# Edge passes of a graph network in pairs of groups, destination addresses loaded mid-step; unpacking's comparisons cut into pieces

## The reference, cut to what matters

```python
for l in range(5):                                   # first network
    h = leaky(x @ W1[l] + b1[l]) @ W2[l] + b2[l]     # a 3125 x 64 table
    e = leaky(edge_attr @ We1[l] + be1[l]) @ We2[l] + be2[l]   # 100000 x 64
    agg = segment_sum(h[src] * e * dot_scale[l], dst, num_segments=n)
    x = layernorm(x + agg * res_w[l]) * ln_g[l] + ln_b[l]
...
msgs = relu(x[src] + edge_inputs)                    # last network
agg = segment_sum(msgs, dst, num_segments=n)
```

## Time and profile before

| | |
|---|---|
| median of 3 runs | 7217.39 us (7210.43 to 7232.62) |
| the profiled execution | 7237.52 us |
| its span | 7235.9 us, mean granted TensorE clock 0.875 |
| unpacking, first to last addition | 1567.4 to 2429.3 us |
| second edge pass, first gather to last scatter | 3031.0 to 3471.1 us |
| last edge pass | 6788.9 to 7215.5 us |

### The profile page before, as it was taken

The page is one execution under the profiler, slowest core; times in us unless marked ns, Lnnn a source line. Parts: engine busy times, 40 slices in busy tenths (PEclk is TensorE's granted clock), DMA queues, the critical chain, the costliest instruction groups (busy, mean ns, idle before and its releaser), DMA issues. The chain is left out here.

```text
span 7235.9 us, 277379 instructions
## 1 busy us (share of the span) xinstructions
PE 5529.5 (76%) x87510; PEld 4589.8 (63%) x87511; DVE 5239.2 (72%) x14769; ACT 2923.1 (40%) x5054; POOL 3176.5 (44%) x4856
## 2 busy tenths in 40 slices
PE   4888888835555477777777777776989998999777
PEld 3666666624444277677676676776957775777676
DVE  7555555589999788788788787887755554555698
ACT  2444444424444434344343343444643332333343
POOL 1777777767777355355354453551000000000254
PEclk9899999955555599899899898997679998999999
DMA  2776766622222488588587786884531111111497
GB/s 73 197 200 200 198 200 200 196 61 73 72 72 72 167 218 228 151 229 229 151 228 202 182 227 157 225 228 148 191 120 64 64 61 41 65 64 65 115 235 203
DMA packets 1403299, 1098.89 MB, mean 152 GB/s; under 512 B 1012405, under 2 KB 1171820, under 8 KB 1393466
## 3 DMA queue, kind: packets, MB, share of 16 engines
q1 hardware_dynamic: 787494, 772.05, 34.5%
q0 software_dynamic: 224768, 240.90, 13.8%
q10 hardware_dynamic: 390804, 82.65, 6.1%
HBM read 815.28 MB, written 278.78 MB: 151 GB/s over the span
## 5 line engine op out<-in xcount | busy, mean ns | idle before, releaser
L542 POOL DMA_DIRECT2D big<-rows x2592 | 1415.8, 546 | 3298.3 <-issue 2332.0
L1328 PE MATMUL ps<-big 128*128 128x64 bf16 x41472 | 1919.5, 194 | 630.7 <-DVE big L1830 286.4
L1328 PEld LDWEIGHTS ps<-big 128*128 128x128 fp8e4 x41472 | 1687.0, 98 | 709.9 <-issue 697.5
L1340 PE MATMUL ps<-big 128*128 128x64 bf16 x20736 | 1734.7, 194 | 11.4 <-issue 5.9
L811 POOL DMA_INDIRECT rows<-big x800 | 1064.8, 1331 | 431.6 <-issue 366.7
L1340 PEld LDWEIGHTS ps<-big 128*128 128x128 bf16 x20736 | 1070.6, 98 | 21.9 <-issue 13.9
L1045 ACT CAST big<-big 128x512 bf16<-128x512 f32 x720 | 445.3, 619 | 909.9 <-DVE big L1843 909.9
L1619 DVE SCALAR_TENSOR_TENSOR big<-big 128x1000 f32<-128x1000 f32 (+1 forms) x300 | 361.7, 1206 | 571.0 <-ACT big L917 559.3
L1288 PE MATMUL ps<-identb,big 128*128 128x128 bf16 x2304 | 444.5, 296 | 394.8 <-DVE big L1731 310.9
L1051 ACT CAST big<-big 128x512 bf16<-128x512 f32 x864 | 534.0, 618 | 459.3 <-issue 342.3
L1239 PEld LDWEIGHTS ps<-big 128*125 128x125 f32 (+1 forms) x4800 | 631.9, 197 | 90.0 <-issue 47.9
(11 more groups left out here) (264 smaller groups left out, 9480.9 us busy)
## 6 DMA issues: line engine op xcount, KB each, us to landing
big<-ohsD SPq DMA_DIRECT2D x432, 512.0 KB, 3.8
big<-ohdD SPq DMA_DIRECT2D x432, 320.0 KB, 4.3
big<-rows POOLq DMA_DIRECT2D x2592, 32.0 KB, 3.7
big<-rows SPq DMA_DIRECT2D x2592, 32.0 KB, 3.6
big<-maskD SPq DMA_DIRECT2D x50, 1600.0 KB, 6.7
big<-rows ACTq DMA_DIRECT2D x1728, 32.0 KB, 3.6
big<-keyT SPq DMA_DIRECT2D x100, 488.3 KB
maskD<-big SPq DMA_DIRECT2D x25, 1600.0 KB, 6.2
```

The costliest lines, as they stand in the source:

```text
L542: eng.dma_start(edge[:, s.r, j, :], rows[bass.ds(v[s.r * (hi - lo) + j - lo], P), col]).then_inc(landed[s.r], 16)
L1328: last = pe.matmul(pG[g.r][:, j * D:(j + 1) * D], ohsR[:, g.r, at:at + P].bitcast(F8), slices[:, g.r, q, (3 * k + c) * D:(3 * k + c + 1) * D],
L1340: last = pe.matmul(pacc[:, bass.ds(w[j], D)], hot[:, g.r, j * P:(j + 1) * P], parts[:, g.r, c, j * D:(j + 1) * D], start=False, stop=False ...
```

## The change

1. **Pairs.** A step of an edge pass takes two groups (`Pair`): 72 steps, in a loop of PR = 4 pairs. Rings hold four pairs, so eight groups. The scatter lags the gather by three pairs. DVE's instructions work on 1024 elements instead of 512.
2. **Parts.** A message stays 32-bit; its upper part is read in place as the upper half of each 32-bit word (`upper_half`: bf16 with a step of two). ACT's two roundings go away; in the last pass ACT does the relu (`rectify`).
3. **Destination one-hots.** DVE makes all sixteen of a pair again (`remake`, through `same`); the store to and the load from `ohdD` go away. Four one-hots are interleaved, so that both inputs of the comparison have runs of four 16-bit values, and `scatter` reads its weights with a step of four elements.
4. **Slices** of the table are copied by ACT, four for a pair, behind ACT's first eight edge DMAs of the pass.
5. **Shares** of the edge rows: SP four tiles of eight, POOL three, ACT one. SP loads 32 addresses in each turn of its loop.
6. **PE's addresses** of the next pair are loaded between the two groups of a step.
7. **Unpacking.** The comparisons of a group are six of 512 elements (two for destinations, four for sources), after additions 0 to 5; after additions 6 and 7 stands none. POOL makes no one-hots, and its identifiers go to a bf16 tile.

```diff
-G_LAG, S_LAG = 1, 5
+PR = 4
+NPAIR = NG // 2
+PT = NPAIR // PR
+S_LAG = 3
-        SP_SHARE, POOL_SHARE, ACT_SHARE = (0, 3), (3, 6), (6, 8)
+        SP_SHARE, POOL_SHARE, ACT_SHARE = (0, 4), (4, 7), (7, 8)
+        def upper_half(v):
+            return v.bitcast(BF16).rearrange("p (a b) -> p a b", b=2)[:, :, 1]
...
+        def load_edges(eng, v, u, lo, hi, col, landed):
+            for k in range(2):
+                for j in range(lo, hi):
+                    at = v[(u.r * 2 + k) * (hi - lo) + j - lo]
+                    eng.dma_start(edge[:, u.r * 2 + k, j, :], rows[bass.ds(at, P), col]).then_inc(landed[u.r], 16)
...
+                def step(u):
+                    if u.r == 0:
+                        hold(sp)
+                        v[:] = starts(SP, u.t, *SP_SHARE, 2 * PR)
+                    if u.live(PR):
+                        sp.wait_ge(m_ready, base + u.lag(PR).i + 1)
+                        hold(sp)
+                    load_hots(u)
+                    load_edges(sp, v, u, *SP_SHARE, col, edge_loaded)
...
+            def slice_tables(u, names):
+                for k in range(4):
+                    last = act.copy(slices[:, 2 * u.r + k // 2, k % 2, :], flat(tabq)[:, bass.ds(names[u.r * 4 + k], 6 * D)])
+                last.then_inc(sliced, 1)
+            def rectify(u, base):
+                if u.lag(2).live():
+                    g = u.lag(2)
+                    act.wait_ge(m_ready, base + g.i + 1)
+                    act.activation(part(g, 0), part(g, 1), ACT.Relu).then_inc(hi_ready, 1)
...
+            def scatter(u, k, j, at):
+                own = hot[:, u.r, (k * 2 + j // QUAD) * QUAD * P:(k * 2 + j // QUAD + 1) * QUAD * P].rearrange("p (d j) -> p j d", j=QUAD)
                 for c in range(3):
-                    last = pe.matmul(pacc[:, bass.ds(w[j], D)], hot[:, g.r, j * P:(j + 1) * P], parts[:, g.r, c, j * D:(j + 1) * D],
+                    f = k * GT * D + j * D
+                    last = pe.matmul(pacc[:, bass.ds(at, D)], own[:, j % QUAD, :], upper_half(part(u, c)[:, f:f + D]),
                                      start=False, stop=False, skip_group_check=True)
...
+            def turn_over(u, v, base, nth):
+                to = u.lag(S_LAG)
+                if u.live(S_LAG):
+                    pe.wait_ge(lo_ready, base + to.i + 1)
...
+                if u.live():
+                    pe.wait_ge(ohs_loaded[u.r], (nth * PT + u.t) * 16 + 16)
+                    pe.wait_ge(sliced, base + u.i + 1)
+                hold(pe)
+                w = halves(v, (W - 1) * D) if u.live(S_LAG) else ()
+                for k in range(2):
+                    for j in range(GT):
+                        if u.live():
+                            got = gather(u, k, j)
+                        if u.live(S_LAG):
+                            put = scatter(to, k, j, w[k * GT + j])
+                    if k == 0 and u.r < PR - 1:
+                        v[:] = blocks(PE, u.i + 1)
...
+            def same(to, local, n):
+                return dve.tensor_tensor(to.rearrange("p (q d j) -> p q d j", q=n, j=QUAD),
+                                         iota4[:, 0:P, :].unsqueeze(1).to_broadcast([P, n, P, QUAD]),
+                                         local.rearrange("p (q j) -> p q j", j=QUAD).unsqueeze(2).to_broadcast([P, n, P, QUAD]), ALU.is_equal)
...
+            def src_hots(t, r, q, k):
+                at = (2 * q + k) * QUAD * P
+                dve.tensor_tensor(ohS[:, r % 2, at:at + QUAD * P].rearrange("p (i j) -> p i j", j=QUAD), iota4[:, k * P:(k + 1) * P, :],
+                                  each(idm[:, r % 2, q * QUAD:(q + 1) * QUAD], P), ALU.is_equal).then_inc(hots_ready, 1)
...
                     if not past(i, NG - 1) or not isinstance(i, int):
-                        one_hots(*chunk(t, r, 1), m)
+                        if m < 2:
+                            dst_hots(*chunk(t, r, 1), m)
+                        elif m < 6:
+                            src_hots(*chunk(t, r, 1), (m - 2) // 2, m % 2)
...
+            def all_pairs(base, kind, nth):
+                def body(u):
+                    message(u, base, kind, nth)
+                    lower(u, base)
+                    remake(u)
+                    rest(u, base, kind)
+                steps(dve, body)
```

More of the change, by code:

```diff
@@ L687, in _, with load_hots @@
             sp.dma_start(x[0:TAIL, W - 1, :], x_in[(W - 1) * P:N, :]).then_inc(ids_loaded, 16)
[L689 to L697, removed]
+            def load_hots(u):
+                sp.dma_start(ohsR[:, 2 * u.r:2 * u.r + 2, :], ohsD[bass.ds(u.i * 2, 2)].rearrange("g p f -> p g f")).then_inc(ohs_loaded[u.r], 16)
@@ L728, in _ @@
+                    load_hots(u)
+                    load_edges(sp, v, u, *SP_SHARE, col, edge_loaded)
+                for r in range(PR):
+                    step(Pair(0, r))
+                with sp.Fori(1, PT) as t:
+                    for r in range(PR):
+                        step(Pair(t, r))
             with sp.Fori(0, LAYERS) as l:
@@ new lines, in edge_pass @@
+            def edge_pass(base, positive, col):
+                v = list(starts(SCALAR, 0, *ACT_SHARE, 2 * PR))
+                for r in range(PR):
+                    load_edges(act, v, Pair(0, r), *ACT_SHARE, col, edge_loaded)
+                names = list(tables_of(SCALAR, 0))
+                def body(u):
+                    if u.live() and u.live(PR):
+                        if u.r == 0:
+                            hold(act)
+                            names[:] = tables_of(SCALAR, u.t)
+                            v[:] = starts(SCALAR, u.t, *ACT_SHARE, 2 * PR)
+                        act.wait_ge(m_ready, base + u.lag(PR).i + 1)
+                        hold(act)
+                    if u.live():
+                        slice_tables(u, names)
+                        if u.live(PR):
+                            load_edges(act, v, u, *ACT_SHARE, col, edge_loaded)
+                    if positive:
+                        rectify(u, base)
@@ L1818, in _ @@
-            names = []
-            def slice_tables(s, base):
-                if s.live(0):
-                    if s.r == 0:
-                        hold(dve)
-                        names[:] = tables_of(DVE, s.t)
-                    if not s.known or s.i >= RING:
-                        dve.wait_ge(gathered, base + s.lag(RING).i + 1)
-                        hold(dve)
-                    for q in range(2):
-                        last = dve.tensor_copy(slices[:, s.r, q, :], flat(tabq)[:, bass.ds(names[s.r * 2 + q], 6 * D)])
-                    last.then_inc(sliced, 1)
@@ L1849, in rest, with remake @@
-            def rest(s, base, kind):
-                if s.live(3):
-                    g = s.lag(3)
-                    dve.wait_ge(hi_ready, base + g.i + 1)
-                    if not g.known or g.i >= 2:
-                        dve.wait_ge(lo_ready, base + g.lag(2).i + 1)
+                        dve.tensor_tensor(part(u, 0), got, own, ALU.mult).then_inc(m_ready, 1)
+                    else:
+                        dve.tensor_tensor(part(u, 1), got, own, ALU.add).then_inc(m_ready, 1)
+            def remake(u):
+                if u.live():
+                    same(hot[:, u.r, :], dstl[:, bass.ds(u.i * 2 * GT, 2 * GT)], 2 * GT // QUAD)
@@ L1886, in _ @@
                 table_parts(l)
-                def body(s):
-                    slice_tables(s, l * NG)
-                    message(s, l * NG, "edge", l)
-                    rest(s, l * NG, "edge")
-                    lower(s, l * NG)
-                    remake(s, l * NG)
-                steps(dve, body)
+                all_pairs(l * NPAIR, "edge", l)
                 lc = Chain(dve, l_chain, l * END)
```

350 lines of the change are left out of this document (116 added, 234 removed).

## The result

The changed kernel takes 7178.65 us (median of 6 runs, 7149.31 to 7196.81) against 7225.92 us (6 runs) on the same chip: a ratio of **0.9925, interval 0.9905 to 0.9944**. By that ratio it is faster by 54 us, by the two medians by 47 us, where 111 us were forecast: a small gain, but clear of the noise. (The ratio is an estimate over the runs; the quotient of the medians is 0.9935.) Its profiled execution took 7184.49 us, its span is 7182.9 us, 53.0 less than before.

What follows compares the result with a forecast made beforehand. SP's issuing queue was taken as the bound of the edge passes, PE close behind. Layers -63, last pass -23 and unpacking -25 gave -111 us: profiled 7126, median 7106 us, own range 7000 to 7210, chance 0.60.

Steps and rivals of the forecast that it cites:

- The bound: Edge passes: SP's issuing queue sets the pace, 5.88 us for a pair against 6.01 before, other engines beside it.
- The layers' -63 us: Five layers' edge passes: each 427.4 us against 440.1, so -12.7 us a layer.
- 68 x 5.88 = 399.8: A layer's pass: after the ring is full, SP has 68 pairs left at 5.88 us each, 399.8 us.
- I take 2.1 us: SP's loop turn, now loading 32 addresses: 2.1 us, bounded by 1.07 and 2.85 us.
- I keep 14.0: End of a layer's pass: 14.0 us from SP's last row to PE's end, kept as before.
- The last pass: Final edge pass: 5.53 us a pair, 72 pairs, ending at 7192 against 7215.5: -23 us.
- The terms given: Unpacking's additions: listed pitches, new against old, put at -0.17 us a group, x 144 = -25 us.
- Rival B: DVE's 16-bit comparisons run at L1815's rate: unpacking +1.6 us a group, +230 us, 7336 us; chance 0.08.
- Rival A: Scatter's strided weights make PE the bound: loads at half pace, 6.33 us a pair, 7399 us; chance 0.10.
- 4.92 us a pair: PE's need in an edge pass: two groups of matmuls plus pauses, 4.92 us, under SP's 5.88.
- Rival C: SP's 32 addresses come in several loads: turn 3.0 to 4.3 us, total 7220 to 7328 us; chance 0.17.
- Rival D: SP's row pitch falls with the traffic, PE paces with 4.92 us: total 6791 us; chance 0.05.

Runs made afterwards that it cites:

- run 1: Changed kernel with the old shares of edge rows (SP three tiles of eight, POOL three, ACT two): 6917.53 us, ratio 0.9559 to the kernel before.
- e12: Changed kernel with the `ohdD` stores put back into unpacking, with DVE's wait for them, nothing reading them: 7166.36 us, ratio 0.9913 to the kernel before.
- e13: Changed kernel, unedited, run again on another chip: 7163.81 us, ratio 0.9926 to the kernel before.
- the first kernel in 6: Changed kernel with ACT's first eight edge rows and slice names loaded ahead of the node part: 7157.68 us, ratio 0.9889 to the kernel before.
- e5: Kernel before with a row moved from SP to ACT (SP two tiles of eight, POOL three, ACT three): 7358.69 us, ratio 1.0175.
- e1: The same run as run 1: changed kernel with the old shares of edge rows, 6917.53 us, ratio 0.9559.

## Why the prediction was right or wrong

**The bound: right.** SP's queue paces a layer's pass of the changed kernel; it has no waits, one row moved off it brings 49 us a layer, and 0.05 us off a row's register work brings 24 to 28. The prediction priced the new shares and found a row more on SP paid for by the other savings; it did not ask what the old ones would give, which was the larger gain.

**A layer's pass: the failed step.** The layers' -63 us rest on "68 x 5.88 = 399.8", and this term was mis-sized; the layers brought some -4 us. From the one-hot load at 3014.12 us, the first after the ring was full, to the end of the last pair's issues at 3425.13 it is 411.0 us, 6.04 a pair. Of the 11.2 us too many:
- some 5.5 us are the long issues of the first pairs (5.98, 5.87, 7.16, 8.53, 6.83 us in place of 5.37, 5.47, 5.37, 7.80, 5.37). The sum had no term for them, although the kernel before has two of 1.09 us and one of 0.72 in its own first groups.
- about 3 us are the turn: "I take 2.1 us" measured 2.43, 16 times, less the seventeenth, which does not lie in this stretch. Most of it is the one instruction that loads the addresses; its first line is of the kernel before, the second of the changed one:

```profile
L535 SPq TENSOR_LOAD <-offs x17: 745/749/770, 3155.6 to 3348.2; - x17
L539 SPq TENSOR_LOAD <-offs x8: 1862/1866/1872, 3161.5 to 3329.6; - x8
```

- about 2.5 us are the pair itself, 5.40 in the mean against 5.35.

The end, "I keep 14.0", measured 15.4 us. The start was as worked out: 6.65 us later (7.1 forecast) and 6.0 us from the first gather to SP (6.5). So 6.65 + 6.0 + 411.0 + 15.4 = 439.1 us against 440.1, not 427.4. The turn, the one term with bounds, stayed within them, and the pair's mean was off by under 3%; but the gain was the small difference of two sums of some 430 us, and 3% of such a sum is the gain. That the forecast's own range, 7000 to 7210, held the result says little: it was four times as wide as the gain.

**The last pass: right.** SP's queue takes 399.9 us for its 72 pairs (6746.14 to 7146.07), 5.55 us a pair (5.53 forecast), though 5.49 in mid-pass and more in the first pairs. The pass gained 24 us inside its window, some 18 with the later start (23 forecast).

**Unpacking.** The size came near (25 forecast, 31 measured), but in part by luck. The terms given (0.77, 0.68, four at 0.67, two at 0.63, against four at 0.75 and four at 0.63) add up to -0.13 us a group and not to -0.17, so to -19 us. The pieces alone took 17, so they were priced well; the rest came from a part that was put at nothing. "POOL's four comparisons and SP's `ohdD` store lay beside this and free nothing" is wrong: without the stores unpacking loses 24 us even with the old comparisons. In the waits of the kernel before (1800 to 2000 us) POOL stood 15.4 us of 200 behind the landing of `ohdD`, a sign that was to be read there:

```profile
POOL big L842 <- DMA ohdD<-big: 15.4, 14, 2.2
```

**The 16-bit comparison.** 2048 elements take 1219 ns and 512 take 418: 0.52 ns an element and some 0.15 us fixed. Rival B is dead. The rule of the Trainium skill ("VectorE: DVE Perf Modes", the perf-mode tier table), two elements a cycle for two 16-bit inputs with a unit step innermost, gave 1.13 us. The rate agrees; the whole took 1.22 us, for the fixed part is 0.15 us and not the 0.07 taken.

**Strided weights.** Rival A did not come: a strided load is 19 ns longer (117 against 98), but the array falls behind by 3 ns, not 29.4. Under SP's pace it is hidden, and where PE paces the contiguous read gave 22 us, with intervals that overlap. The Trainium skill ("TensorE: Matmul & The Clock Gate", on fast weight load) says that weights are read 32 bits at a time. From this the prediction worked out a halved pace for a step of four; no run here shows it.

**PE.** 4.92 us a pair was forecast; run 1, where it paces, takes 5.03. The load in mid-step shows a pause of 0.03 us (0.35 taken), and the turn one of 1.02 us (1.2 taken); but nine matmuls take 0.275 us instead of 0.265, which is 0.16 us a pair, and the rest is spread over small pauses. Rival C, a turn of 3.0 us or more, did not come (2.43). Rival D, a pitch that falls with the traffic, did not come: the kernel moves 165 GB/s in the pass instead of 220, and SP's row in a layer costs 0.57 us against 0.58.

**What stays open.** What makes single issues long was not tried, but the kept trace has a suspect. From the first gather to the last scatter of the five layers' passes 43 of SP's issues are longer than 0.5 us. Of these, 38 overlap a packet of the DMA queue that carries instructions, and those packets, about 1 us each and ten to twelve a pass, cover 2.5% of that time. In the kernel before it is 15 of 31. From 3020 to 3050 us six of them stand in the view of the DMA queues (packets, MB, share), from 3150 to 3180 none:

```profile
q8 instruction: 6, 0.10, 1.4%
```

That fits issues held up while the loop's code is loaded; no run takes the packets away, so it is not shown as the cause. Open too is what makes SP take now 4.29, now 4.36 us for the same eight rows: the two runs on one chip whose passes are unedited, `e12` and `e13`, have 86 ns of register work and 333 ns for the issue of a row, the first profile and the runs on the other chips 91 and 337. No run takes the pairs, the deeper rings and the dropped `ohdD` loads apart, and the gain of the first kernel in 6 is not settled either.

## What to carry to other kernels

Where transfers are issued by three queues, balance them anew after every change that frees an engine: here the engine freed was ACT, the row went to SP, and undoing that one line made 0.9925 into 0.9559. Among the runs that compute the same values none was better by more than the noise. A queue without waits was the bound here, and its price is the register work of each issue and each load of addresses; both can be read from its timeline and from the duration of the load, if its growth with the number of addresses is allowed for. Before issues are moved to another place in an engine's program, ask who waits for that engine there. And where a forecast gain is the difference of two long sums, work out what 3% of the sum is before trusting it.

## What the runs showed of the hardware

A load of addresses grows with their number. On SP it took 0.524 us for 8 (`e5`), 0.749 for 12 (the kernel before), 1.424 for 24 (`e1`) and 1.866 for 32 (the changed kernel), medians between 3150 and 3350 us: 0.056 us for each address and some 0.08 besides. The whole turn cost 1.07 us with 12 and 2.43 with 32.

PE's pause at the loop's turn costs clock. After 3.32 us without a matmul in the changed kernel the granted clock falls to half (1.2 GHz) from 3168.59 to 3172.00, and six gathers take 0.51 us where 0.34 are usual:

```profile
3168.10 0.34 PE L1287 MATMUL ps<-big 128*128 128x64 bf16 x6 [3.32 <-ACT big L1004]
...
3169.28 0.51 PE L1287 MATMUL ps<-big 128*128 128x64 bf16 x6
...
3172.10 0.34 PE L1287 MATMUL ps<-big 128*128 128x64 bf16 x6
```

That is why the layer's window shows a clock of 0.94 after and 0.99 before. While SP paces this is hidden. In run 1, where the pause at the turn is 1.02 us, the granted clock of the second pass stays at full from 3010.2 us to 3334.4.
